# A two-layer attention and feed-forward kernel: the first batch of the second attention moved ahead of the mixture's last batch, all places worked out anew

## The chip, the core and the metric

The kernel runs on one core of one Trainium2 chip. The metric is the time of one execution on the device, in microseconds, from the median of several runs. The work runs on five engines that each have their own queue and meet only through semaphores: TensorE (PE, with PEld for its weight loads), VectorE (DVE), ScalarE (ACT), GpSimd (POOL) and SyncE (SP), which here only issues DMAs.

## What is computed

Four blocks are added onto x, one after the other, each on a layer norm of x:

```python
# x, ctx: (8 batches, 128 tokens, 128 channels)
x = x + L0_xattn(layernorm(x), ctx, ctx)      # attention over channels, 4 heads, twice (global, local)
x = x + L0_ffn(layernorm(x))                  # "mixture": 16 experts weigh q, k, v and the output
x = x + L1_xattn(ctx, layernorm(x), ctx)      # "second attention": 16 heads of 8 channels over 128 tokens
x = x + L1_ffn(layernorm(x))                  # 8 experts (2 best of a router) and a shared one

# L0_ffn, of one batch: rw = weights of the 16 experts for each token
q, k, v = sum_e rw[e] * (h @ {q,k,v}_proj[e])
attn = softmax(causal(q @ k.T / 8)) @ v
out = sum_e (attn * rw[e]) @ o_proj[e]

# L1_xattn, of one batch: for each of 16 heads
out = concat_h softmax(q_h @ k_h.T / sqrt(8)) @ v_h;  out = out @ Wc.T + bc
```

## The kernel before

All data stays in SBUF. Work goes batch by batch (b = 0 to 7), and the last block goes by 28 chunks of 128 hidden rows (14 chunks for each half of the batches). The program is one list for each engine, and each list is made by the same loop over a step counter, `for s in range(LAST)`: a function is emitted on an engine where its place says so. A step is no time: it only orders what one engine does. Waits on semaphores do the rest, and an engine that waits holds everything behind it in its list.

The places come from small functions. `at_mix(b, u)` is step 32 b + u of the mixture of batch b, less `MIX_EARLY[b]`. `at_att(b, u)` is step 8 (35 + 2 b) + u of the second attention of batch b, less `ATT_EARLY[b]`; `at_score` does the same for its first scores. `at_once(u)` is step u, for the rest of the first block. `at_tail` places the router, `at_first` the first two chunks of the feed-forward.

The functions that the text speaks of, in the order in which a batch meets them:

- Mixture. `scale_hidden` (L1099, DVE) multiplies the normalised x with the weights of four experts, `project` (L1476, PE, one at steps 0, 8, ... 248, so 32 of them) makes q, k, v. Then `take_qkv` (ACT), `turn_qk` (L1486, PE), `take_qkT` (L658, ACT), `scores2` (L1491, PE), `softmax2_max` (DVE), `exp2` (L665, ACT), `softmax2_norm` (DVE), `turn_p` (L1500, PE), `take_pT` (L672, ACT), `attend2` (L1504, PE), `take_aT` (L678, ACT), `mix` (L1131, DVE), `project_o` (L1514, PE), `after_mixture` (L1135, DVE), `rstd_of` (L488, POOL), `normalise` (L881, DVE).
- Queries of the second attention. `turn_x3` (L1525, PE), `take_xn3T` (L684, ACT), `project_q` (L1529, PE), `split_q` (DVE), `turn_q` (L1534, PE), `take_qs` (L690, ACT).
- Second attention. `scores3` (L1549, PE, two for each batch), `softmax3` (L1144, DVE, only the maxima), `split_m` (DVE), `mark_queries` (L1559 and L1562, PE), `take_marked` (L705, ACT), `turned_scores` (L1576, PE, two for each batch), `exp3` (L700, ACT, two), `attend3` (L1589, PE), `take_y` (L711, ACT), `turn_y` (L1596, PE), `divide` (DVE), `turn_divided` (L1602, PE), `take_yT` (L717, ACT), `bring_x` (L1611, PE), `project_c` (L1615, PE), `after_attention` (DVE), `take_x3` (L721, ACT), `rstd_of`, `normalise`.
- Router and feed-forward. `turn_x4`, `router`, `turn_w`, `up` (L1657, PE), `silu` (L765 or L769, ACT), `hidden` (DVE), `high_hidden` (ACT), `split_hidden` (L533, POOL), `down` (L1713, PE). Their weights are split into a high and a low part while the mixture runs: `high_weights` (L737 to L739, ACT) and `split_weights` (L533, POOL), one of 14 chunks every 8 steps from step 8 W4.

PSUM has eight banks, PB[0] to PB[7], and mixture and second attention use the same ones: PB[1] holds q and k turned, the mixture's scores and the marked queries; PB[3] holds the turned p, attend2, attend3, turned y and divided y; PB[5] holds project_o and project_c. Waits keep the order in which the two may use them. Before the change every such wait says that all eight batches of the mixture are through with the bank, for instance:

```python
def attend3(b):
    pe.wait_ge(ex_ready, 2 * b + 2)
    pe.wait_ge(vm_ready, b + 1)
    if b == 0:
        pe.wait_ge(aT_ready, NB)
    else:
        pe.wait_ge(yT_ready, b)
```

The two `turned_scores` of a batch write the same pair of banks, so the second waits until `exp3` has read the first.

## Time and profile before

| what | us |
|---|---|
| runs of the kernel before | 238.11, 235.94, 236.2 (median 236.2) |
| the profiled execution, its own time | 236.62 |
| its span, first to last instruction | 234.8 |
| PE busy | 211.8 |
| DVE, ACT, POOL busy | 166.5, 112.5, 95.3 |

### The profile page before, as it was taken

What the parts mean: (1) busy time and instruction counts of PE and PEld (TensorE: products, weight loads), DVE (VectorE), ACT (ScalarE), POOL (GpSimd) and SP (SyncE); (2) the same over time, 40 slices, a digit from 0 to 9 for tenths busy, and PEclk for the clock granted to TensorE, in tenths of its full rate; (3) what the DMA queues carried; (4) which work ended last, traced back from release to release, by engine and by line L of the source; (5) the groups of instructions that cost most, each with busy time, mean ns of one, the idle gap of its engine ahead of it and who ended that gap; (6) DMA issues with size and microseconds to landing.
All of it is one profiled execution on the core that took longest, in us unless ns stands there. A gap on an engine that the chain in (4) does not pass through costs nothing.

```text
span 234.8 us, 4985 instructions
## 1 busy us (share of the span) xinstructions
PE 211.8 (90%) x1767; PEld 180.2 (77%) x1767; DVE 166.5 (71%) x495; ACT 112.5 (48%) x259; POOL 95.3 (41%) x127
## 2 busy tenths in 40 slices
PE   1398669999999999999799999998699999999994
PEld 0356549999999998988579888887577887888872
DVE  3598797669977989858792687865765688265753
ACT  0435432423264462422263777678453745555552
POOL 7143100150096999810411021122336655655660
PEclk9999957999999999999976999999999999999998
DMA  6997000398199953300300000000024430163401
GB/s 188 349 419 228 3 6 0 96 289 155 60 260 245 242 190 89 81 12 0 89 4 0 3 3 0 3 4 0 3 48 89 122 101 6 42 189 133 152 27 45
DMA packets 19256, 23.33 MB, mean 99 GB/s; under 512 B 1792, under 2 KB 12192, under 8 KB 19104
## 3 DMA queue, kind: packets, MB, share of 16 engines
q1 hardware_dynamic: 18896, 22.94, 34.3%
q8 instruction: 14, 0.23, 0.4%
q10 hardware_dynamic: 336, 0.08, 0.2%
q14 instruction: 10, 0.08, 0.1%
HBM read 22.39 MB, written 0.62 MB: 98 GB/s over the span
## 4 chain that ended last, share of the span: by engine, by line
PE 83%; DVE 7%; ACT 3%; DMA 2%; issue 2%; ACTq 1%; POOL 0%; DVEq 0%
PE psum L1476 19%; PE psum L1657 17%; PE psum L1713 8%; PE psum L1514 7%; PE psum L1576 3%; PE psum L1589 3%; PE psum L1549 3%; DMA kv<-kv_dram 2%; PE psum L1386 2%; PE psum L1342 2%; PE psum L1491 1%; PE psum L1534 1%; PE psum L1562 1%; PE psum L1596 1%; PE psum L1504 1%
## 5 line engine op out<-in xcount | busy, mean ns | idle before, releaser
L488 POOL TENSOR_TENSOR rstd<-ve,m 128x1 f32<-128x1 f32 (+1 forms) x20 | 14.2, 712 | 96.9 <-DVE ve L872 96.8
L1476 PE MATMUL psum<-wqkv,hm 128*128 128x192 f32 x256 | 47.8, 335 | 0.0
L533 POOL TENSOR_TENSOR qs<-hm,qs 128x512 fp32r<-128x512 f32 (+1 forms) x26 | 33.9, 1302 | 22.3 <-ACT qs L746 22.1
L1476 PEld LDWEIGHTS psum<-wqkv,hm 128*128 128x128 f32 x256 | 42.3, 195 | 0.1
L1144 DVE TENSOR_REDUCE negm<-psum 128x8 f32<-128x1024 f32 x16 | 19.6, 1222 | 7.7 <-PE psum L1549 7.6
L1713 PE MATMUL psum<-qs,wdhi 128*128 128x512 f32 (+1 forms) x56 | 21.8, 401 | 0.1
L1212 DVE TENSOR_TENSOR hm<-hm,psum 128x512 f32<-128x512 f32 x19 | 13.0, 686 | 11.3 <-POOL qs L533 5.0
L700 ACT ACTIVATE exT<-psum 128x1024 f32<-128x1024 f32 x16 | 16.4, 1024 | 7.5 <-PE psum L1576 7.0
L1099 DVE TENSOR_TENSOR hm<-xn2T,exT 128x512 f32<-128x512 f32 x24 | 19.6, 817 | 0.1
L746 ACT ACTIVATE qs<-hm 128x512 fp32r<-128x512 f32 (+1 forms) x28 | 17.5, 627 | 3.3 <-DVE hm L1215 2.0
L765 ACT ACTIVATE psum<-psum 128x512 f32<-128x512 f32 x19 | 11.1, 583 | 16.5 <-PE psum L1657 16.3
L1514 PE MATMUL psum<-wo,mixT 128*128 128x128 f32 x128 | 17.4, 295 | 0.1
L1514 PEld LDWEIGHTS psum<-wo,mixT 128*128 128x128 f32 x128 | 16.6, 209 | 0.3 <-issue 0.2
L1215 DVE TENSOR_TENSOR hm<-hm,psum 128x512 f32<-128x512 f32 x19 | 13.1, 688 | 2.0
L1713 PEld LDWEIGHTS psum<-qs,wdhi 128*128 128x128 f32 (+1 forms) x56 | 10.5, 188 | 3.4 <-DVE qs L1231 0.9
L1131 DVE TENSOR_TENSOR mixT<-aT,rwm 128x1024 f32<-128x1024 f32 x8 | 10.5, 1317 | 2.8 <-issue 1.5
L1657 PE MATMUL psum<-x4hi,wahi 128*128 128x512 f32 (+1 forms) x28 | 12.0, 427 | 0.0
L1576 PE MATMUL psum<-qs,ks 32*128 32x128 f32 x128 | 10.8, 287 | 1.1 <-ACT qs L705 0.9
L1713 PE MATMUL psum<-qs,wdlo 128*128 128x512 f32 (+1 forms) x28 | 11.1, 397 | 0.0
L1657 PE MATMUL psum<-x4lo,wahi 128*128 128x512 f32 (+1 forms) x28 | 11.1, 396 | 0.0
L1657 PE MATMUL psum<-x4lo,wbhi 128*128 128x512 f32 (+1 forms) x28 | 11.1, 395 | 0.0
L1657 PE MATMUL psum<-x4hi,wblo 128*128 128x512 f32 (+1 forms) x28 | 11.0, 393 | 0.0
(235 smaller groups left out, 487.8 us busy)
## 6 DMA issues: line engine op xcount, KB each, us to landing
exT<-rw_rows SPq DMA_DIRECT2D x24, 256.0 KB, 4.8
rwm<-rw_rows SPq DMA_DIRECT2D x16, 256.0 KB, 5.8
hm<-ww_rows SPq DMA_DIRECT2D x7, 256.0 KB, 3.3
wqkv<-wqkv_dram SPq DMA_DIRECT2D x1, 1536.0 KB, 10.5
hm<-ww_rows SPq DMA_DIRECT2D x4, 224.0 KB, 3.3
wa<-wa_dram SPq DMA_DIRECT2D x1, 880.0 KB, 12.9
wb<-wb_dram SPq DMA_DIRECT2D x1, 880.0 KB, 13.3
wdn<-wdn_dram SPq DMA_DIRECT2D x1, 832.0 KB, 15.0
```

What stands on the lines that cost most here:

```text
L488: nc.gpsimd.tensor_tensor(dst, src, m16[:, 0:src.shape[1]], ALU.pow).then_inc(signal, 1)
L533: return nc.gpsimd.tensor_tensor(dst, src, hi.bitcast(F32), ALU.subtract)
L700: nc.scalar.activation(exT[:, b % 2, 2 * p:2 * p + 2, :], turned_pair, ACT.Exp).then_inc(ex_ready, 1)
L746: nc.scalar.activation(hhi[0:n, k % 3, :], hid[0:n, k % 3, :], ACT.Copy).then_inc(hhi_ready, 1)
L1099: V.tensor_tensor(hm[:, b % 2, 4 * q:4 * q + 4, :], bc(xn2T[:, b, :], 1, 4), weights, ALU.mult).then_inc(hm_ready, 1)
L1144: V.tensor_reduce(negm[:, b % 2, 2 * p:2 * p + 2, :], score_pair.rearrange("p j (g k) -> p j g k", g=4), AX.X, ALU.max, negate=True).then_ ...
L1215: V.tensor_tensor(hid[:, k % 3, :], hid[:, k % 3, :], PB[gate_bank(k)][:, :], ALU.mult).then_inc(hid_ready, 1)
L1476: last = mm(bank[:, 0:3 * HD], hm[:, b % 2, e, :], wqkv[:, e, :], start=(e == 0), stop=(e == E0 - 1))
L1514: last = mm(PB[5][:, 0:C], mixT[:, r, :], wo[:, r, :], start=(r == 0), stop=(r == E0 // 2 - 1))
L1576: last = mm(PB[turned_score_bank(j)][:, T * g:T * g + T], ks[quarter(j), b, g, :], qs[quarter(j), b, g, :], start=True, stop=True)
L1657: last = mm(bank[0:n, :], w[:, c0:c0 + n], x[:, cols4], start=(j == 0), stop=(j == 2))
L1713: last = mm(bank[:, :], w[0:n, ch, :], h[0:n, k % 3, :], start=(ch == 0 and j == 0), stop=(ch == NCH - 1 and j == 2))
```

## The change

It keeps all instructions and alters their places and some waits. The mixture's last batch (7) and the second attention's first batch (0) change turns in the banks that they share: attention 0 now needs only seven batches of the mixture, and batch 7 of the mixture waits for attention 0 (`turn_qk` for `take_marked`, `turn_p` for `take_yT`, `project_o` for `take_x3`).

```diff
-W4 = 13
+W4 = 16
-MIX_EARLY = (0, 0, 0, 0, 0, -8, 4, -4)
-SCORE_EARLY = (88, 56, 12, 4, 4, 4, 4, 4)
-ATT_EARLY = (0, 0, 0, 0, 0, 0, 0, 0)
+MIX_EARLY = (0, -8, -16, -8, -12, -8, 4, -4)
+SCORE_EARLY = (92, 44, 12, 4, 4, 4, 4, 4)
+ATT_EARLY = (40, 0, 0, 0, 0, 0, 0, 0)
-SECOND_EARLY = 16
+SECOND_EARLY = 8
...
             def exp3(h):
...
                 if h == 0:
+                    act.wait_ge(hm_ready, 4 * NB - 4)
+                if h == 2:
                     act.wait_ge(hm_ready, 4 * NB)
...
             def turn_qk(b):
...
                 if b >= 1:
                     pe.wait_ge(s2_ready, b)
+                if b == NB - 1:
+                    pe.wait_ge(qm_ready, 1)
                 else:
                     pe.wait_ge(partsT_ready, 1)
...
             def turn_p(b):
...
+                if b == NB - 1:
+                    pe.wait_ge(yT_ready, 1)
                 pe.wait_ge(pn_ready, b + 1)
...
             def project_o(b):
...
+                if b == NB - 1:
+                    pe.wait_ge(x3_ready, 1)
                 pe.wait_ge(mix_ready, b + 1)
...
             def mark_queries(b):
                 if b == 0:
+                    pe.wait_ge(s2_ready, NB - 1)
+                else:
                     pe.wait_ge(s2_ready, NB)
-                else:
                     pe.wait_ge(qm_ready, b)
...
             def attend3(b):
...
                 if b == 0:
+                    pe.wait_ge(aT_ready, NB - 1)
+                else:
                     pe.wait_ge(aT_ready, NB)
-                else:
                     pe.wait_ge(yT_ready, b)
...
             def bring_x(b):
                 if b == 0:
+                    pe.wait_ge(x2_ready, NB - 1)
+                else:
                     pe.wait_ge(x2_ready, NB)
-                else:
                     pe.wait_ge(x3_ready, b)
...
-                    if s == at_att(b, 40):
+                    if s == at_att(b, 42):
                         attend3(b)
...
-                    if s == at_tail(hf, 128, 176):
+                    if s == at_tail(hf, 108, 174):
                         turn_w(hf)
```

Some sixty places (the number u in `at_...(b, u)`) change in the same way as the last two. The mixture of batches 1 to 4 comes 8 to 16 steps later, and that of batches 5 to 7 stays; attention 0 comes 40 steps earlier; in the tail `mark_queries(7)` now stands ahead of `router(0)`, `turn_w(0)` ahead of `bring_x(6)` instead of behind `project_c(7)`, and on ACT `router_softmax(0)` stands ahead of `take_yT(5)`. On POOL, the mixture's `rstd_of` for batch 4 now stands ahead of the last three `split_weights`; before it stood behind all 14.

**The order on PE behind the last `project`.** First the list before, from `project_o(6)` to the second `turned_scores(0)`. L1514 is project_o, L1525 turn_x3, L1529 project_q, L1559 and L1562 mark_queries, L1500 turn_p, L1549 scores3, L1576 turned_scores, L1504 attend2, L1534 turn_q.

```order
L1514 MATMUL psum<-wo,mixT 128x128 x8
L1525 MATMUL psum<-ident,xna 128x128
L1529 MATMUL psum<-wattn,xn3T 128x128
L1559 MATMUL psum<-qs,identr 128x512
L1562 MATMUL psum<-identr,msp 128x128 x4
L1500 MATMUL psum<-ident,pn 128x128
L1549 MATMUL psum<-ks,qs 128x128 x8
L1576 MATMUL psum<-qs,ks 128x128 x8
L1504 MATMUL psum<-pT,v 128x128
L1534 MATMUL psum<-ident,qsp 128x128 x4
L1549 MATMUL psum<-ks,qs 128x128 x8
L1576 MATMUL psum<-qs,ks 128x128 x8
```

Now the list of the changed kernel, whose PE lines are some ten numbers higher, from the first `turned_scores(0)` to `turn_divided(0)`: L1585 is turned_scores, L1510 attend2, L1495 scores2, L1542 turn_q, L1522 project_o, L1599 attend3, L1533 turn_x3, L1606 turn_y, L1537 project_q, L1612 turn_divided, L1506 turn_p.

```order
L1585 MATMUL psum<-qs,ks 128x128 x8
L1510 MATMUL psum<-pT,v 128x128
L1495 MATMUL psum<-qkT 128x128
L1585 MATMUL psum<-qs,ks 128x128 x8
L1542 MATMUL psum<-ident,qsp 128x128 x4
L1522 MATMUL psum<-wo,mixT 128x128 x8
L1599 MATMUL psum<-exT,vm 32x128 x16
L1533 MATMUL psum<-ident,xna 128x128
L1606 MATMUL psum<-ident,ysb 128x128 x4
L1537 MATMUL psum<-wattn,xn3T 128x128
L1612 MATMUL psum<-ident,yq 128x128
L1506 MATMUL psum<-ident,pn 128x128
```

Before, `mark_queries(0)` and the rest of attention 0 came behind `project_o(6)`; now both `turned_scores(0)` come ahead of it, and `attend3(0)`, `turn_y(0)` and `turn_divided(0)` ahead of `turn_p(7)`.

**The order on ACT at the same place.** Before, from `take_qs(4)` on: L690 is take_qs, L658 take_qkT, L665 exp2, L684 take_xn3T, L705 take_marked, L672 take_pT, L700 exp3, L678 take_aT.

```order
L690 ACTIVATE qs<-psum 128x512
L658 ACTIVATE qkT<-psum 64x256
L665 ACTIVATE pn,den<-s,nmx 128x128
L684 ACTIVATE xn3T<-psum 128x128
L705 ACTIVATE qs<-psum 128x512
L672 ACTIVATE pT<-psum 128x128
L700 ACTIVATE exT<-psum 128x1024
L678 ACTIVATE aT<-psum 128x128
```

In the changed kernel, from `take_xn3T(4)` on: L684 is take_xn3T, L658 take_qkT, L702 exp3, L678 take_aT, L690 take_qs, L713 take_y, L665 exp2, L719 take_yT, L672 take_pT.

```order
L684 ACTIVATE xn3T<-psum 128x128
L658 ACTIVATE qkT<-psum 64x256
L702 ACTIVATE exT<-psum 128x1024
L678 ACTIVATE aT<-psum 128x128
L702 ACTIVATE exT<-psum 128x1024
L690 ACTIVATE qs<-psum 128x512
L713 ACTIVATE ysb<-psum 128x512
L665 ACTIVATE pn,den<-s,nmx 128x128
L684 ACTIVATE xn3T<-psum 128x128
L719 ACTIVATE yT<-psum 128x128
L672 ACTIVATE pT<-psum 128x128
```

`take_qkT(7)` no longer stands behind `take_qs(4)`, and both `exp3(0)` and `take_y(0)` now stand ahead of `exp2(7)`.

## Rows read from the trace of the kernel before

**Rows 1.** The page's part 1: busy time of each engine.
```profile
PE 211.8 (90%) x1767; PEld 180.2 (77%) x1767; DVE 166.5 (71%) x495; ACT 112.5 (48%) x259; POOL 95.3 (41%) x127
```

**Rows 2.** Busy time by stretch: stretch, length, busy and instructions of each engine, granted clock.
```profile
core 0: us, PE busy (x) PEld busy (x) DVE busy (x) ACT busy (x) POOL busy (x), PEclk, DMA share, GB/s
24.00:38.70 14.70, 10.60 (x58) 9.08 (x59) 11.54 (x53) 4.76 (x11) 1.01 (x1) 0.65 0.01 3
38.70:106.00 67.30, 67.30 (x480) 63.21 (x479) 53.94 (x154) 26.86 (x105) 37.33 (x59) 1.00 0.59 150
106.00:120.60 14.60, 12.55 (x110) 10.57 (x108) 11.70 (x33) 5.47 (x16) 3.50 (x6) 1.00 0.16 37
120.60:127.40 6.80, 6.43 (x32) 5.82 (x30) 3.42 (x9) 1.79 (x3) 0.00 (x0) 0.50 0.00 1
127.40:134.00 6.60, 6.33 (x118) 5.37 (x116) 4.08 (x10) 4.80 (x7) 0.84 (x2) 1.00 0.01 2
134.00:158.00 24.00, 23.64 (x348) 20.50 (x349) 17.68 (x48) 18.28 (x31) 3.95 (x10) 1.00 0.01 2
158.00:176.00 18.00, 15.43 (x150) 12.03 (x150) 12.08 (x50) 11.11 (x23) 5.82 (x8) 1.00 0.08 15
176.00:232.00 56.00, 55.52 (x251) 44.02 (x249) 35.53 (x70) 30.16 (x55) 32.49 (x25) 1.00 0.31 91
```

**Rows 3.** PE's instructions in order of time: start, us, line, count, idle time before.
```profile
105.72 1.47 PE L1476 MATMUL psum<-wqkv,hm 128*128 128x192 f32 x8
...
112.62 0.48 PE L1491 MATMUL psum<-qkT 64*128 64x128 f32 x2 [0.95 <-ACT qkT L658]
...
159.54 0.66 PE L1576 MATMUL psum<-qs,ks 32*128 32x128 f32 x8 [0.65 <-ACT qs L705]
...
165.58 1.08 PE L1589 MATMUL psum<-exT,vm 128*32 128x128 f32 x32 [1.01 <-ACT yT L717]
```

**Rows 4.** The chain that ended last, in order of time: start, us, what.
```profile
113.18 2.04 PE psum L1514 x16
...
117.44 0.59 PE psum L1549 x8
...
123.36 3.52 PE psum L1514 x16
...
132.98 1.01 PE psum L1589 x32
...
143.50 0.59 PE psum L1576 x8
...
145.87 0.42 PE psum L1611 x2
146.28 0.22 PE psum L1615 x2
```

**Rows 5.** ACT's instructions in order of time, same columns as rows 3.
```profile
111.71 0.60 ACT L690 ACTIVATE qs<-psum 128x512 fp32r<-128x512 f32 x1 [0.16 <-PE psum L1534]
112.20 0.37 ACT L658 ACTIVATE qkT<-psum 64x256 f32<-64x256 f32 x1
...
118.78 1.02 ACT L700 ACTIVATE exT<-psum 128x1024 f32<-128x1024 f32 x1 [0.67 <-PE psum L1576]
...
128.84 0.60 ACT L711 ACTIVATE ysb<-psum 128x512 f32<-128x512 f32 x1
```

**Rows 6.** DVE's costliest groups from 70 to 98 us: xcount, busy, mean ns.
```profile
L1099 DVE TENSOR_TENSOR hm<-xn2T,exT 128x512 f32<-128x512 f32 x13 | 11.8, 905 | 0.0
L1131 DVE TENSOR_TENSOR mixT<-aT,rwm 128x1024 f32<-128x1024 f32 x3 | 4.4, 1467 | 1.5 <-issue 1.5
```

**Rows 7.** The same view from 99 to 122 us.
```profile
L1131 DVE TENSOR_TENSOR mixT<-aT,rwm 128x1024 f32<-128x1024 f32 x3 | 3.7, 1221 | 0.3 <-ACT aT L678 0.3
```

**Rows 8.** POOL's last low part of the weights, from the instructions in order of time.
```profile
98.02 0.90 POOL L533 TENSOR_TENSOR wdlo<-wdn,wdhi 96x128 fp32r<-96x128 f32 x1
```

More of the change, by code:

```diff
@@ L782, in _ @@
                     take_ks(4)
-                if s == at_once(8):
+                if s == at_once(0):
                     take_ks(5)
-                if s == at_once(16):
+                if s == at_once(0):
                     take_ks(6)
-                if s == at_once(24):
+                if s == at_once(30):
                     take_ks(7)
-                if s == at_once(16):
+                if s == at_once(32):
                     take_x1(1)
-                if s == at_once(17):
+                if s == at_once(3):
                     wide_marks()
-                if s == at_once(40):
+                if s == at_once(50):
                     take_xn2T(1)
-                if s == at_once(88):
+                if s == at_once(84):
                     take_rwT(1)
                 for b in reversed(range(NB)):
+                    if s == at_mix(b, 30):
+                        take_qkv(b)
                     if s == at_mix(b, 32):
-                        take_qkv(b)
-                    if s == at_mix(b, 40):
                         take_qkT(b)
-                    if s == at_mix(b, 58):
+                    if s == at_mix(b, 54):
                         exp2(b)
-                    if s == at_mix(b, 74):
+                    if s == at_mix(b, 66):
                         take_pT(b)
@@ L807, in _ @@
                         take_aT(b)
[L808 removed]
+                    if s == at_mix(b, 118):
                         take_xn3T(b)
[L810 removed]
+                    if s == at_mix(b, 134):
                         take_qs(b)
[L812 removed]
+                if s == at_once(64):
                     gate_exp(1)
@@ L1256, in _ @@
                     channel_softmax(1)
-                if s == at_once(1):
+                if s == at_once(0):
                     turn_heads(1)
-                if s == at_once(16):
+                if s == at_once(20):
                     after_channels(1)
-                if s == at_once(24):
+                if s == at_once(36):
                     normalise(xnb, 1, HALF, NB, 4, xn2_ready)
-                if s == at_once(24):
+                if s == at_once(26):
                     norms(1)
-                if s == at_once(48):
+                if s == at_once(56):
                     gate(1, 0)
-                if s == at_once(56):
+                if s == at_once(58):
                     gate(1, 1)
-                if s == at_once(64):
+                if s == at_once(66):
                     gate(1, 2)
-                if s == at_once(72):
+                if s == at_once(66):
                     gate(1, 3)
-                if s == at_once(80):
+                if s == at_once(68):
                     gate(1, 4)
                 for b in range(NB):
-                    if s == at_score(b, 4):
+                    if s == at_score(b, 0):
                         softmax3(2 * b)
-                    if s == at_score(b, 14):
+                    if s == at_score(b, 12):
                         softmax3(2 * b + 1)
@@ L1725, in _ @@
                     turn_keys(4)
-                if s == at_once(8):
+                if s == at_once(0):
                     turn_keys(5)
-                if s == at_once(16):
+                if s == at_once(24):
                     turn_keys(6)
@@ L1731, in _ @@
                     turn_keys(7)
-                if s == at_once(16):
+                if s == at_once(22):
                     attend_channels(1)
-                if s == at_once(40):
+                if s == at_once(48):
                     turn_x2(1)
-                if s == at_once(48):
+                if s == at_once(52):
                     gate_logits(1)
-                if s == at_once(88):
+                if s == at_once(82):
                     turn_rw(1)
@@ L1750, in _ @@
                         project_o(b)
+                    if s == at_mix(b, 120):
+                        turn_x3(b)
                     if s == at_mix(b, 122):
-                        turn_x3(b)
-                    if s == at_mix(b, 126):
                         project_q(b)
-                    if s == at_mix(b, 140):
+                    if s == at_mix(b, 136):
                         turn_q(b)
```

59 lines of the change are left out of this document (28 added, 31 removed).

## Prediction

> **What bounds the kernel now.** I read the busy times first: PE 211.8 of 234.8 us, DVE 166.5, the others half or less [rows 1]. So the end is set by PE's work and by the time in which PE waits or runs slowly. Then the busy time by stretch [rows 2]: from 38.7 to 106 us (30 of the 32 `project`) and from 176 us on PE is never or hardly idle (67.30 of 67.30, 55.52 of 56.00). A reordering can gain nothing there, and loses only if another engine falls behind. Three stretches are left.
>
> 1. From 24 to 38.7 us PE is busy 10.60 of 14.70 us at a mean clock of 0.65. The change leaves the code ahead of the loop as it is and alters little in these steps.
> 2. From 106 to 134 us, between the last `project` and the steady second attention: PE waits 2.05 + 0.37 + 0.27 = 2.7 us, and from 120.6 to 127.4 its clock is 0.50, that is 1.2 GHz. One `project_o` takes 3.52 us there against 2.04 earlier [rows 4].
> 3. From 158 to 176 us, router and first chunks: 18.00 - 15.43 = 2.6 us idle. The largest waits are 0.65 for `take_marked(7)` and 1.01 for `take_yT` [rows 3].
>
> Between these, 134 to 158 us, PE is busy 23.64 of 24.00. So the change must be judged by stretches 2 and 3.
>
> **Up to the last `project`.** Before, it starts at 105.72 [rows 3]. Three of the four `scores3` of batches 0 and 1 had been done by then, after the change two, so one piece of 0.59 [rows 4] moves behind: the last `project` starts at about 105.13. The mixture of batches 1 to 4 is 8 to 16 steps later there, but its work on PE is the same, and other work fills the place. The cover for this is DVE: from 38.7 to 106 it is busy 53.94 of 67.30, and while POOL splits weights it is slower: `mix` takes 1.47 against 1.22 us without it [rows 6, 7]. POOL's last split ended at 98.9 [rows 8]. It will now end at about 110: `rstd_of` for batch 4 must wait for `project_o(4)`, which I place at 101, and three chunks of about 1.8 us, an `rstd_of` and an `add_bc` follow. So `mix(5)` and the last `scale_hidden` run at the slow price (0.905 us) [rows 6]. I count it in the waits below, and take 0 for the stretch itself; if the cover fails, each late `scale_hidden` shows as a wait of PE of some tenths.
>
> **Stretch 2, the work.** Before, from 105.72 to the end of `attend3(1)` at 132.98 + 1.01 = 133.99 are 28.3 us. Of these 2.7 are waits, and the slow clock costs half of the 6.80 - 0.37 us that PE was busy under it, 3.2 us. At full clock 22.4 us of work are left. After the change the same span of the list holds one more `scores3` (0.59), and `bring_x(0)` and `project_c(0)` come ahead of `attend3(1)` (0.42 + 0.22) [rows 4]: 23.6 us. With W for the waits and K for the clock, `attend3(1)` ends at 105.13 + 23.6 + W + K = 128.7 + W + K. The kernel before has come equally far at 133.99 + 0.64 = 134.6. So the difference is W + K - 5.9.
>
> **The waits W.** I set PE's new list out in order, with these prices, beside the lists of ACT and DVE with theirs. One wait of before goes: `scores2(7)` waited 0.95 us [rows 3], as `take_qkT(7)` (0.37) stood behind `take_qs(4)` (0.60) on ACT [rows 5]; it no longer does. But attention 0 brings its own chain without the company of other batches:
> - `mark_queries(0)` waits for `split_m(0)`, which stands behind `mix(5)` at the slow price: 0.3.
> - The second `turned_scores(0)` waits until `exp3` has read the banks (1.02) [rows 5], with only `attend2(6)` and `scores2(7)` between: 0.6.
> - `project_o(6)` waits for `mix(6)`, behind `softmax3(3)` and `split_q(4)` on DVE: 0.4.
> - `turn_y(0)` stands all but directly behind `attend3(0)` and waits for `take_y` (0.60) [rows 5]: 0.7. Behind it on ACT stands `exp2(7)`, though its input is there, and `take_xn3T(5)`, so `project_q(5)` waits 0.4 more.
> - `turn_divided(0)` 0.2, then `turn_p(7)`, by the new wait on `yT_ready`, 0.45: behind it stand `scores3(4)` and all the rest of PE, which need nothing of it.
> - `turn_q(5)`, `turn_x3(6)`, `project_o(7)` (`mix(7)` behind `softmax3(4)`, `after_attention(0)` and `split_m(1)` on DVE; the new wait on `x3_ready` is over by then), the next `turned_scores`: 0.15, 0.3, 0.5, 0.15 and 0.35.
>
> The sum is 4.5 us, an estimate worked out from those rows; hops of 0.04 to 0.1 us may be off, so I keep 3.5 to 5.5. The lower bound for a list that did what it is meant to would be the 2.7 of before. So the change removes one long wait and adds several short ones, +1.8 us net.
>
> **The clock K.** Before, PE's clock fell at 120.6 after a stretch with 12.55 of 14.60 us busy, its longest wait 0.95 us. By my placing, the new list from 106 to 120.6 has waits of 0.3, 0.6, 0.4, 0.7, 0.4, 0.2 and 0.45, that is 3.05 us against 2.05, the most of it at its end. So I expect the fall again, at about the same time and for as long: 6.8 us at half rate lose 3.4 us. The later waits of the list (0.15, 0.3, 0.5, 0.15, 0.35) vanish under the slower PE, as the other engines don't slow down: K = 3.4 - 1.4 = 2.0. If it lasts half as long, 1.7 - 0.7 = 1.0. The bounds are 0 (no fall) and what the start of the kernel shows: 14.70 us at a mean of 0.65 are 10.3 us at half rate, 5.15 us, less some 2.2 of waits, K = 2.9.
>
> Stretch 2 then gives 4.5 + 1.0 to 2.0 - 5.9 = -0.4 to +0.6, and I take +0.1.
>
> **Stretch 3.** `mark_queries(7)` ahead of `router(0)` ends the 0.65 wait. On the other side `attend3(6)` needs `take_yT(5)`, which now stands behind `router_softmax(0)` on ACT, and that waits for the router's maxima on DVE: 0.7 for 0.65. `take_yT(6)` still stands behind the first `silu`, about 1.0 as before. `turn_divided(7)` now stands ahead of `up(1)` and waits 0.8 for `divide(7)`, where `up(1)` used to cover; `turn_w(0)` out of the way early gives some of it back. Before 2.6 us idle, now 2.0 to 3.4: I take -0.2 for the stretch with a range of -0.7 to +0.8. From `up(4)` on all is as before and PE-bound.
>
> The sum against the profiled execution is 236.62 + 0.1 - 0.2 = 236.5; the profile lies 0.4 above the median 236.2, so by the median the forecast is 236.1, in round numbers 236.0. A measurement of this kernel can tell about 1% (2.4 us) from no change.
>
> **The rivals.**
> - *The clock does not fall.* K = 0 gives -1.4 - 0.2 = -1.6: 234.6. With W at 3.5 and the tail at its best it is 233.1, beyond 1%. For it: the new waits are each shorter than the 0.95 that goes. Against it: their sum is larger, and before it was no long wait either that led to the fall.
>   The Trainium skill, "TensorE: Matmul & The Clock Gate", section "HAM oscillation — how this bites in real kernels", has the clock fall after long idle gaps of PE. By that rule neither list would lose the clock, and this case would follow. The trace does not agree: the clock fell to 0.50 at 120.6 with no wait over 0.95 us ahead.
> - *The planner's list does better than mine.* W stays at the 2.7 of before and the clock holds: 2.7 - 5.9 = -3.2 in stretch 2, 236.2 - 3.2 - 0.2 = 232.8. For it: attention 0 and the chains of batches 5 to 7 are independent, so there is work to fill with. Against it: the list puts `turn_y(0)` where only one small turn stands between it and its `attend3`.
> - *Slower.* The thin stretch makes the clock fall sooner and stay low as long as at the start (10.3 us): 4.5 + 2.9 - 5.9 = +1.5, with the waits at 5.5 +2.5, with the tail at its worst +3.3: 237.7 to 239.5. It decides as soon as PE's idle time between 110 and 120 is over 3 us. For it: 0.7, 0.4, 0.2 and 0.45 follow one another within 4 us. Against it: `project_o(6)` and `attend3(0)`, 2.8 us without a wait, come right before.
>
> **How the numbers follow.** The forecast 0.42, within 1%. The clock holds 0.20, of which 0.07 is beyond 1%. The better list 0.22, all beyond. Slower 0.16, of which 0.13 is beyond. So faster 0.29, same 0.42 + 0.13 + 0.03 = 0.58, slower 0.13. The range that leaves 2 in 10 out goes from 232.8 to 238.2; the forecast's own range is 235.0 to 237.2.
>
> **What the changed profile would show.** The last `project` at about 105.1 with no PE wait ahead of it; POOL's last split near 110 and `mix(5)` at 1.4 us; no wait of `scores2(7)`; waits of PE on `exp3`, `take_y` and `take_yT` of batch 0 of 0.4 to 0.7 us; the clock at 0.50 for some 6.8 us from about 120; `attend3(1)` ending at 133.2 + 1.0 to 2.0; 2.0 to 3.4 us idle in the tail. The forecast is wrong if the clock stays at 1.00 from 106 on, if PE waits for `scale_hidden` before 105 us, or if the waits behind the last `project` sum to 3 us or less.

## The result, and the profile after

| kernel | median, us | lowest to highest | ratio to the kernel before |
|---|---|---|---|
| before | 236.41 | 235.94 to 238.11, 4 runs | 1 |
| changed | 241.14 | 240.38 to 256.72, 4 runs | 1.0179 [1.0123, 1.0235] |
| changed, measured again (f1 below) | 240.86 | 235.95 to 257.43, 12 runs | 1.0048 [0.9978, 1.0119] |

The change makes the kernel slower, by 4.7 us in the first comparison and by 3.6 us between the medians of the second. Medians are over all executions, while the ratios leave out those over 1.5% above the kernel's fastest, so the two need not agree: the low ratio of the second row rests on three of the 12 executions (235.95 and 236.38 us at a mean granted clock of 0.985, 238.64 us at 0.971). That spread is a part of the story.

The profiled execution took 241.07 us, its span is 239.3 us (before 236.62 and 234.8). The page's busy times, to be held against [rows 1]:

```profile
PE 217.7 (91%) x1766; PEld 183.8 (77%) x1767; DVE 165.1 (69%) x495; ACT 111.7 (47%) x259; POOL 93.5 (39%) x127
```

The instructions are the same, yet PE is busy 5.9 us longer: 4.5 us of span, and 1.4 us less idle. DVE, ACT and POOL are not busier. So it is not that PE waits more; it is busy for longer with the same work. Now busy time by stretch, the counterpart of [rows 2], with the tail cut where the clock changes:

```profile
core 0: us, PE busy (x) PEld busy (x) DVE busy (x) ACT busy (x) POOL busy (x), PEclk, DMA share, GB/s
24.00:38.70 14.70, 11.68 (x56) 10.12 (x57) 10.49 (x49) 3.67 (x8) 1.01 (x1) 0.55 0.02 3
38.70:106.00 67.30, 66.42 (x468) 62.61 (x468) 52.67 (x156) 27.28 (x106) 32.06 (x51) 1.00 0.57 150
106.00:134.00 28.00, 25.36 (x259) 21.15 (x260) 20.61 (x53) 11.87 (x29) 8.12 (x18) 1.00 0.08 20
134.00:158.00 24.00, 24.00 (x350) 20.10 (x340) 16.87 (x41) 16.91 (x28) 3.52 (x9) 1.00 0.01 2
...
161.50:169.00 7.50, 7.24 (x54) 6.04 (x55) 3.44 (x21) 4.10 (x6) 0.55 (x1) 0.54 0.01 2
```

The clock holds at 1.00 behind the last `project`, where it was at 0.50 from 120.6 to 127.4 before. Instead it is at 0.50 for some 3.4 us longer at the start (0.55 on average against 0.65), and for 6.8 us near 162. The marks of PE, to be held against [rows 3]:

```profile
106.46 1.47 PE L1478 MATMUL psum<-wqkv,hm 128*128 128x192 f32 x8
...
133.41 1.08 PE L1599 MATMUL psum<-exT,vm 128*32 128x128 f32 x32
...
161.76 1.79 PE L1599 MATMUL psum<-exT,vm 128*32 128x128 f32 x32 [0.63 <-ACT yT L719]
...
170.16 1.08 PE L1599 MATMUL psum<-exT,vm 128*32 128x128 f32 x32 [0.84 <-ACT yT L719]
...
173.46 0.33 PE L1612 MATMUL psum<-ident,yq 128*128 128x128 f32 x1 [0.85 <-DVE yq L1167]
```

L1599 is `attend3`, here of batches 1, 6 and 7; it took 1.79 us at the half clock and 1.08 at the full one. And the piece that shows what the forecast missed, in the steady second attention, first before, then after. L1549 and L1557 are `scores3`, L1576 and L1585 the second `turned_scores` of the batch, L1611 and L1622 `bring_x`.

```profile
145.03 0.44 PE L1549 MATMUL psum<-ks,qs 32*128 32x128 f32 x4
145.21 0.33 PE L1576 MATMUL psum<-qs,ks 32*128 32x128 f32 x2
145.31 0.28 PE L1549 MATMUL psum<-ks,qs 32*128 32x128 f32 x2
145.37 0.27 PE L1576 MATMUL psum<-qs,ks 32*128 32x128 f32 x2
145.42 0.27 PE L1549 MATMUL psum<-ks,qs 32*128 32x128 f32 x2
145.48 0.38 PE L1576 MATMUL psum<-qs,ks 32*128 32x128 f32 x4
145.80 0.49 PE L1611 MATMUL psum<-xr,ident 128*128 128x128 f32 x2
```

```profile
145.37 0.66 PE L1557 MATMUL psum<-ks,qs 32*128 32x128 f32 x8
145.96 0.49 PE L1622 MATMUL psum<-xr,ident 128*128 128x128 f32 x2
146.37 0.66 PE L1585 MATMUL psum<-qs,ks 32*128 32x128 f32 x8
146.96 0.49 PE L1626 MATMUL psum<-wattn,yT 128*128 128x128 f32 x2
```

Before, the two groups of eight 32x128 matmuls, which use different quarters of the array's rows, stand next to each other in the list and run mixed, in 0.77 us for both (145.03 to 145.80). After, `bring_x`, which uses the whole array, stands between them, and each takes its own 0.59 us. `attend3` follows `attend3` after 4.95 us before (144.02, 148.96, 153.91) and after 5.54 us now (144.35, 149.89, 155.42).

The Trainium skill, "TensorE: Matmul & The Clock Gate", section "Part 3: Packing small matmuls — row/col tiling", says that matmuls on different row strips of the array run together, but start and end strictly in program order. The rows agree with the running together. They don't agree with the order of the starts: all eight `scores3` stand ahead of the eight `turned_scores` in the list, yet four of them start at 145.31 and 145.42, after the first `turned_scores` at 145.21. So that order isn't what keeps the second group back here; what the rows show is that it starts behind `bring_x` where `bring_x` stands between.

### The profile page after: what moved, and what is told of

It reads as the page before. It is cut to its first block, busy times and chain, and to the rows that moved or that the text cites. A ratio compares the mean times of both kernels' runs of the same rounds, so it can differ in the third digit from the quotient of the medians.

```text
span 239.3 us, 4993 instructions
## 1 busy us (share of the span) xinstructions
PE 217.7 (91%) x1766; PEld 183.8 (77%) x1767; DVE 165.1 (69%) x495; ACT 111.7 (47%) x259; POOL 93.5 (39%) x127
## 4 chain that ended last, share of the span: by engine, by line
PE 83%; DVE 8%; issue 3%; ACT 3%; DMA 2%; ACTq 1%; DVEq 0%
PE psum L1668 17%; PE psum L1478 16%; PE psum L1724 8%; PE psum L1522 6%; PE psum L1599 4%; PE psum L1585 4%; PE psum L1557 3%; DMA kv<-kv_dram 2%; PE psum L1344 2%; PE psum L1606 2%; PE psum L1388 1%; PE psum L1542 1%; PE psum L1622 1%; PE psum L1571 1%; PE psum L1495 1%
## 5 line engine op out<-in xcount | busy, mean ns | idle before, releaser
L702 ACT ACTIVATE exT<-psum 128x1024 f32<-128x1024 f32 x16 | 16.4, 1024 | 9.3 <-PE psum L1585 8.7
L1101 DVE TENSOR_TENSOR hm<-xn2T,exT 128x512 f32<-128x512 f32 x24 | 17.9, 752 | 0.5 <-DMA exT<-rw_rows 0.5
L1522 PE MATMUL psum<-wo,mixT 128*128 128x128 f32 x128 | 15.9, 277 | 0.3 <-DVE mixT L1133 0.3
L1522 PEld LDWEIGHTS psum<-wo,mixT 128*128 128x128 f32 x128 | 15.1, 192 | 0.8 <-issue 0.5
L1133 DVE TENSOR_TENSOR mixT<-aT,rwm 128x1024 f32<-128x1024 f32 x8 | 10.2, 1270 | 4.2 <-ACT aT L678 3.1
L1585 PE MATMUL psum<-qs,ks 32*128 32x128 f32 x128 | 11.0, 292 | 0.6 <-ACT exT L702 0.3
L1668 PE MATMUL psum<-x4hi,wbhi 128*128 128x512 f32 (+1 forms) x28 | 11.2, 401 | 0.0
L1668 PE MATMUL psum<-x4hi,walo 128*128 128x512 f32 (+1 forms) x28 | 11.2, 401 | 0.0
```

What stands on the lines that cost most here:

```text
L702: nc.scalar.activation(exT[:, b % 2, 2 * p:2 * p + 2, :], turned_pair, ACT.Exp).then_inc(ex_ready, 1)
L1101: V.tensor_tensor(hm[:, b % 2, 4 * q:4 * q + 4, :], bc(xn2T[:, b, :], 1, 4), weights, ALU.mult).then_inc(hm_ready, 1)
L1522: last = mm(PB[5][:, 0:C], mixT[:, r, :], wo[:, r, :], start=(r == 0), stop=(r == E0 // 2 - 1))
L1585: last = mm(PB[turned_score_bank(j)][:, T * g:T * g + T], ks[quarter(j), b, g, :], qs[quarter(j), b, g, :], start=True, stop=True)
L1668: last = mm(bank[0:n, :], w[:, c0:c0 + n], x[:, cols4], start=(j == 0), stop=(j == 2))
```

## The experiments

Each row of this table is one profiled execution, cut at four marks read from PE's instructions in order of time: A the start of the last `project`, B 1.01 us after the start of `attend3(1)` (its end at full clock), C the start of `attend3(6)`, D the start of `up(4)`, E the span's end. The last column says where the clock was at 0.50, and for how long. Several have up to 2 us more of that at the span's end, not listed. The profile of i3 is left out: its execution took 246.33 us, 9.7 us over the median of its kernel, with the clock at 0.50 for 27 us between 121 and 152 us.

| profile | A | A to B | B to C | C to D | D to E | clock at 0.50, us |
|---|---|---|---|---|---|---|
| before | 105.72 | 28.20 | 26.21 | 15.97 | 58.70 | start 10.2, from 120.6 6.8 |
| changed | 106.46 | 27.96 | 27.34 | 18.40 | 59.14 | start 13.7, from 162 6.8 |
| f1_after_again | 104.38 | 27.97 | 27.33 | 15.37 | 59.15 | start 6.8 |
| e1_pair_back | 105.44 | 27.98 | 25.94 | 16.73 | 59.11 | start 10.2, from 161 3.4 |
| e2_pair_broken | 107.00 | 25.23 | 27.73 | 15.99 | 58.75 | start 13.7 |
| e3_tail_back | 105.03 | 27.98 | 28.06 | 15.96 | 58.67 | start 6.8 |
| e4_mid_only | 107.61 | 27.97 | 28.00 | 15.89 | 58.83 | start 13.7, from 156 3.4 |
| f2_fill_before | 106.75 | 25.23 | 26.22 | 18.71 | 58.79 | start 13.7, from 159 6.8 |
| f3_fill_tail | 106.67 | 27.97 | 28.66 | 17.36 | 59.24 | start 13.7, from 162 3.4 |
| f4_before_tail | 106.72 | 25.24 | 28.38 | 21.04 | 59.12 | start 13.7, from 158.5 13.7 |
| h1_fill_start | 104.95 | 26.76 | 26.22 | 18.91 | 58.66 | from 120 3.4, from 158 6.8 |
| h2_qkT_ahead | 104.67 | 25.24 | 26.21 | 18.66 | 58.92 | start 6.8, from 156.5 6.8 |
| h3_both | 104.43 | 25.25 | 26.22 | 18.68 | 58.72 | from 156.5 6.8 |
| i1_hold_before | 104.06 | 28.08 | 26.12 | 16.14 | 60.10 | from 118.5 6.8 |
| i2_hold_after | 104.12 | 29.09 | 27.32 | 15.38 | 60.49 | from 113 3.4 |
| j1_full_before | 104.68 | 25.17 | 26.13 | 16.14 | 58.68 | none |
| j2_full_pair | 105.13 | 27.89 | 27.94 | 15.07 | 59.27 | from 132 3.4 |

My theory after the result: the order itself costs about 3 us, and the clock's falls land where they do in each execution. The rival: the order is nearly neutral, and the changed kernel loses by making the clock fall more.

**e1_pair_back.** The changed kernel with the pair together again, all but batch 0.

```diff
-                    if s == at_att(b, 32):
+                    if s == at_att(b, 32 if b == 0 else 28):
                         turned_scores(2 * b + 1)
```

> The changed kernel, with the second turned_scores of batches 1 to 7 on PE 4 steps earlier again, so that it follows scores3 directly and bring_x comes behind both. Theory A (the two sets of small matmuls, on different quarters of the array, ran side by side in the kernel before: 0.77 us for both against 0.59 + 0.59 apart, and the period of a batch went from 4.95 to 5.54 us where bring_x parts them): three batches get 0.5 to 0.6 us back each, so about 1.7 us faster than the changed kernel, 239.4 us, periods of attend3 4.95 us. Theory B (PE is not what sets the period there): the period stays 5.5 us and the time 241.

Median 238.62 us (before 237.09 in the same job), ratio 1.0045 [1.0005, 1.0086]. B to C is 25.94 against 27.33 in f1, both at full clock: 1.4 us.

**e2_pair_broken.** The reverse, in the kernel before, for three batches.

```diff
-                    if s == at_att(b, 28):
+                    if s == at_att(b, 32 if b in (3, 4, 5) else 28):
                         turned_scores(2 * b + 1)
```

> The kernel before, with the second turned_scores of batches 3, 4 and 5 put 4 steps later on PE, so that bring_x parts it from scores3. Theory A: 3 times 0.5 to 0.6 us slower, about 238.1 us, periods of attend3 5.5 us in place of 4.95. Theory B: no change, 236.4.

B to C is 27.73 against 26.21: 1.5 us for three pairs. The whole is 1.0063 [0.9981, 1.0145], too coarse alone. The rows show the same separate groups as in the changed kernel:

```profile
149.21 0.66 PE L1549 MATMUL psum<-ks,qs 32*128 32x128 f32 x8
149.80 0.49 PE L1611 MATMUL psum<-xr,ident 128*128 128x128 f32 x2
150.22 0.66 PE L1576 MATMUL psum<-qs,ks 32*128 32x128 f32 x8
```

Done and undone give the same size, so this term is shown. The medians agree with it less well: 237.29 us in place of the 238.1 expected. The profile also shows the clock at 1.00 all through A to B, in the old order, and with that A to B takes 25.23 us and not 28.20.

**e3_tail_back.** The changed kernel with the router and the first chunks at their old places, in the manner of

```diff
-SECOND_EARLY = 8
+SECOND_EARLY = 16
...
-                    if s == at_tail(hf, 108, 174):
+                    if s == at_tail(hf, 128, 176):
                         turn_w(hf)
```

> The changed kernel with all places of the router and of the first two feed-forward chunks (on every engine) as before the change. Theory T (the new places of the tail make the waits that let the clock fall at 161 us): the clock stays up there, 2 to 3 us faster than the changed kernel, 238.5 us. Theory P (when the clock falls depends on what PE did in the stretch ahead, which is thin in both): it falls in the tail again and the time is within 0.7 us of 241.1.

Median 239.3, 1.0081 [1.0038, 1.0123]. No fall came in the tail of this one profile. C to D is 15.96 as before, D to E 58.67 as before. But `turn_x4(0)` now waits 1.32 us for `normalise`, so B to C grows to 28.06: the `rstd_of` ahead of it had ended at 152.95, but on DVE `normalise` kept its new place, behind the next `softmax3` and `split_m`, and began at 154.93. Of the tail this says only that its new places change D to E by +0.45.

**e4_mid_only.** Pair, tail and the rest of the first block back; the moved attention and the mixture's places stay.

> The changed kernel with the pairs restored and the head and tail places of the kernel before: of the change only the exchange of batch 7 and batch 0 and the places of mixture and second attention are left. If each part costs by itself: 241.1 - 1.7 (pairs) - 1 (head) - 2.4 (tail) = 236.0. If the fall of the clock in the tail stays: 238.4.

Median 239.81, 1.006 [1.0018, 1.0101], above both expectations, so adding up the parts did not give it. Here too `turn_x4(0)` waits 1.3 us for `normalise`. A to B is 27.97, as in every other unfilled profile with the moved attention, whatever stood around it. The 2.7 us over 25.23 belong to the part of the change that is left here: the exchange of attention 0 and batch 7, with the new places of mixture and second attention.

**f1_after_again.** The changed kernel, unaltered.

> The changed kernel once more, unaltered. What it settles is which of its marks are fixed and which move between executions. Theory (the order costs, the clock is added to it): from the last project to the end of attend3(1) 28.0 us again, attend3 periods of 5.54 us in the steady part again, whatever the clock does; the stretch at 0.50 at the start between 6.8 and 13.7 us long; a second stretch at 0.50 near 160 us of 3.4 or 6.8 us. Median 239 to 241 us. Rival (most of the loss was one unlucky placing of the clock's falls): the median of the new executions comes within 1.5 us of the kernel before.

A to B and B to C repeat to 0.01 us. No fall came in the tail this time, and C to D took 15.37 us against 18.40. So the order is fixed and the falls are not. The 12 executions go from 236 us at a mean clock of 0.985, over 238.6 to 240.3 at 0.971, to 241.4 to 241.9 at 0.957, and two took 257 us at 0.886. The kernel before took 235.4 and 236.7 at 0.971 and 237.7 at 0.957 in that job, so at an equal mean clock the changed kernel is 3.6 to 4 us slower on average.

**f2_fill_before.** The kernel before with the 0.95 us wait of `scores2(7)` filled.

```diff
+            def fill(bank, n):
+                for i in range(n):
+                    tr(PB[bank][:, 384:512], wattn[:, 2, :], ident[:, :])
+
             def scores2(b):
+                if b == NB - 1:
+                    pe.wait_ge(x2_ready, NB - 2)
+                    fill(5, 7)
```

> The kernel before, with seven turns of 0.11 us into a free bank put ahead of scores2(7), where PE waited 0.95 us. The turns' results are never read. If short idle times of PE between 106 and 120 us are what brings its clock to 0.50 at about 120, the clock now stays at 1.00 there, and last project to the end of attend3(1) takes 25.2 us as in the run e2_pair_broken, not 28.2; the median comes 1.5 to 3 us below the kernel before. If the fall has nothing to do with that wait, it comes as before in most executions, and the median stays within 0.5 us.

Median 237.28, 1.001 [0.9973, 1.0046]. No fall came at 120, but e2 had none either, and one came at 159 instead, where the first profile had none. The median met the second expectation, but one filled wait settles nothing.

**f3_fill_tail.** The changed kernel with `fill` ahead of `attend3(6)` and `attend3(7)`, into the bank of `project_c`.

> The changed kernel with five turns ahead of attend3(6), which waited 0.63 us for take_yT, and eight ahead of attend3(7), which waited 0.84 us; the turns' results are never read. If these waits bring the clock to 0.50 from 162 to 169 us, it now holds, and attend3(6) to up(4) takes 15.0 to 15.5 us, not 18.4: the median comes 2 to 3.4 us below the changed kernel. If the clock falls whatever PE does in those waits, attend3(6) to up(4) stays at 16.7 to 18.4 us.

Median 241.44, 1.0166 [1.0108, 1.0224]. This one failed as a test: to write that bank, `fill` itself had to wait for `take_x3`, 0.71 us, so it came behind the idle time and not into it.

```profile
162.04 1.33 PE L1590 MATMUL psum<-ident,wattn 128*128 128x128 f32 x5 [0.71 <-ACT xr L723]
163.30 1.08 PE L1606 MATMUL psum<-exT,vm 128*32 128x128 f32 x16
```

**f4_before_tail.** The kernel before with the new places of the router and the first chunks.

> The kernel before with only the changed places of the router and of the first chunks. If the new tail's own waits bring the clock down, it shows a stretch at 0.50 beginning between 158 and 163 us, and attend3(6) to up(4) takes 16.7 to 18.4 us against 15.97; from up(4) to the end 0.4 us more than before. If the fall near 162 us came from the moved attention and the parted pairs ahead of it, it doesn't fall here, attend3(6) to up(4) takes about 15.0 us, and the whole is 0.5 us below to 0.5 us above the kernel before.

Median 242.45, 1.021 [1.014, 1.028]: worse than either kernel. A fall of 13.7 us came from 158.5 on, but that isn't the test that was meant: `turned_scores(14)` waits 2.03 us, as `take_marked(7)` kept its old place and so stands behind the moved `router_softmax(0)` on ACT. The new tail places only fit the new attention places, so this run can't tell what they are worth alone.

**h1_fill_start.** The kernel before with PE's idle time between 20 and 33 us filled.

```diff
-            add_rows(PB[5], R_BP)
-            add_x(1)
+            fill(5, 22)
             sum_queries(1)
+            fill(5, 5)
             turn_x2(0)
+            fill(5, 6)
...
             turn_keys(1)
+            fill(5, 5)
             turn_keys(2)
             turn_keys(3)
+            add_rows(PB[5], R_BP)
...
             turn_rw(0)
+            add_x(1)
```

> The kernel before with PE's idle times between 20 and 33 us filled: 38 turns of 0.11 us into a bank that is not used yet, and the bias rows and x of the second half put into that bank after them, later than before. The turns' results are overwritten, never read. If idle time of PE is what brings its clock to 0.50 at 25 to 29 us in every profile so far, the stretch at 0.50 at the start goes or shrinks to at most 3.4 us, the last project starts at 103 to 104.5 instead of 105.7 to 107.0, and the median is 1.5 to 3 us below the kernel before, if no other fall takes its place. If the fall does not depend on these idle times, it stays 6.8 to 13.7 us long and the time is the same or up to 1 us more.

The fall at the start is gone. That stretch, and the one in which the clock fell later:

```profile
24.00:38.70 14.70, 12.51 (x93) 9.75 (x91) 11.99 (x53) 4.96 (x11) 1.01 (x1) 1.00 0.02 4
...
158.00:176.00 18.00, 16.18 (x128) 12.64 (x129) 9.46 (x35) 9.51 (x19) 4.19 (x5) 0.81 0.04 10
```

All ten other profiles up to here and h2 had 6.8 to 13.7 us at 0.50 at the start; none of the seven filled there (h1, h3, i1 to i3, j1, j2) had any. So idle time of PE brings that fall. But the median is 236.63 us against 236.61, 0.9998 [0.9952, 1.0044]: what the start gave (`project` at 104.95, not the 103 to 104.5 expected, against 105.72) went again in falls at 120 and 158, where 3.4 us of fall cost 1.5 us (A to B 26.76 against 25.23) and at the start 1.1. At the start PE is busy 10.60 of 14.70 us [rows 2], so a slower PE has idle time to use up; that this is the reason is not shown.

**h2_qkT_ahead.** The kernel before, with the one wait ended that the change does remove.

```diff
-                    if s == at_mix(b, 40):
+                    if s == at_mix(b, 40 if b < NB - 1 else 37):
                         take_qkT(b)
```

> The kernel before with take_qkT(7) placed ahead of take_aT(6) and take_qs(4) on ACT, which alone ends the 0.95 us wait of scores2(7), the one wait of this stretch that the change does remove. If that wait was on the path, from the last project to the end of attend3(1) it takes 24.3 to 24.6 us at full clock, not 25.23, and the median is 0.6 to 0.9 us below the kernel before. If other waits grow by as much (attend2(6) for take_aT(6), mark_queries(0) for take_qs(4)), the stretch keeps its 25.2 us.

Median 236.2, 1.0014 [0.9974, 1.0053]. A to B keeps its 25.24 us. `scores2(7)` does not wait, and the next instruction waits 1.09 us for `mix(6)` on DVE:

```profile
110.54 0.48 PE L1491 MATMUL psum<-qkT 64*128 64x128 f32 x2
112.12 1.13 PE L1514 MATMUL psum<-wo,mixT 128*128 128x128 f32 x8 [1.09 <-DVE mixT L1131]
```

So the longest wait of the stretch was worth nothing. It stood ahead of one as long that it hid.

**h3_both.** h1 and h2 together.

> Both edits together, as a candidate that beats both kernels. If each works as its theory says: 2 to 4 us below the kernel before, last project at 103 to 104.5 us, and attend3(1) ended 24.5 us later. If neither matters: within 0.5 us of it.

Median 237.33 us, 0.7 above the kernel before in the same job (236.61) and not 2 to 4 below it. The ratio of 0.9903 [0.9835, 0.9972] rests on 4 of its 12 executions. One execution held the clock at 1.00 throughout and took 232.5 us, less than any execution of either kernel.

**i1_hold_before, i2_hold_after, i3_hold_pair.** h3 with `fill` also ahead of `project_o(6)`, `turned_scores(14)`, `attend3(7)` and `bring_x(7)`; the changed kernel with the start filled as in h1 and `fill` ahead of `attend3(6)`, `attend3(7)` and `turn_divided(7)`; and that one with the edit of e1. The banks are ones whose last reader is through, so `fill` adds no wait that lasts:

```diff
             def attend3(b):
 
                 pe.wait_ge(ex_ready, 2 * b + 2)
+                if b == NB - 2:
+                    pe.wait_ge(mx3_ready, NU)
+                    fill(4, 5)
+                if b == NB - 1:
+                    fill(0, 7)
                 pe.wait_ge(vm_ready, b + 1)
```

> The run h3_both with PE's four longest waits after the start filled too: eight turns ahead of project_o(6), five ahead of turned_scores(14), eight ahead of attend3(7), five ahead of bring_x(7), all into banks that nobody reads then. If idle time of PE brings every fall, the clock now stays at 1.00 nearly everywhere in most executions, attend3(6) to up(4) takes 16.0 us instead of 18.7, and the median is 232 to 234 us, 3 to 4 us below the kernel before and below its own fastest executions. If the falls come anyway, only elsewhere, the median stays at 236 to 237 us.

> The changed kernel with the same filling of the start, and turns ahead of attend3(6), attend3(7) and turn_divided(7) into banks that are free without a new wait. With the clock's falls out of both, the difference to i1_hold_before is the order alone: my theory says 3.4 us (2.7 behind the last project, 1.1 in the steady attention, 0.4 from up(4) on, less 0.2 ahead of the last project and 0.6 in the tail), that is 236 us with the clock held. The rival, that the changed kernel is slower because it lets the clock fall more, says less than 1.5 us between the two.

> The same with the second turned_scores of each batch but the first put back to its place ahead of bring_x. Theory: attend3(1) to attend3(6) 1.4 us shorter than in i2_hold_after (25.9 us against 27.3), and the whole 1.4 us below it, still 2 us above i1_hold_before. If the parted pairs only looked dear because the clock or a wait moved with them, the two have the same median.

Medians 237.77 (0.9948 [0.9892, 1.0003]), 239.36 (1.01 [1.0068, 1.0133]) and 236.66 us (0.9958 [0.9923, 0.9993]), with the kernel before at 237.08. So i1 missed its 232 to 234 us. No fall came in the filled tail; with the old order and tail and no filling there it had come four times in six (f2, h1, h2, h3; not before and e2). A fall that began at 113 or 118.5 took its place, behind waits of 0.24 to 0.37 us that were still unfilled. The pair's term is there in the whole time: 2.7 us between i2 and i3. That is more than 1.4, and the rest has its own row: in i1 and i2, not in i3, PE stands still once for 1.1 us while waiting for nothing that the profile shows, and D to E is 1.4 us longer (60.10 against 58.68 in j1).

```profile
207.28 1.05 PE L1747 MATMUL psum<-ident,xr 128*128 128x128 f32 x8
209.41 0.47 PE L1685 MATMUL psum<-x4hi,wahi 128*128 128x512 f32 x1 [1.08 <-issue]
```

What that is stays open. Between the medians of i1 and i2 lie 1.6 us, where 3.4 were expected for the order and less than 1.5 by the rival. With falls left in both and this standstill in both profiles, that settles neither.

**j1_full_before, j2_full_pair.** i1 with three turns more ahead of `project_q(4)`, (5) and (6); i3 with two to four ahead of `turned_scores(1)`, `project_o(6)`, `turn_y(0)`, `turn_divided(0)` and `turn_p(7)`.

```diff
             def project_q(b):
+                if b == 4:
+                    pe.wait_ge(x2_ready, 5)
+                    fill(5, 3)
+                if b in (5, 6):
+                    pe.wait_ge(aT_ready, b + 2)
+                    fill(3, 3)
                 pe.wait_ge(xn3T_ready, b + 1)
```

> i1_hold_before with three turns each ahead of project_q(4), (5) and (6), where PE waited 0.37 us each time, so that hardly any idle time of PE between 20 us and 176 us is left unfilled. If idle time brings the fall that i1_hold_before had at 118.5 us, the clock is 1.00 from the first to the last but a few us, the mean at least 0.99 in most executions, and the median 232.5 to 234 us. If falls come at about 120 us although PE is hardly idle there, idle time is not the whole cause, and the median stays near 237 us.

> i3_hold_pair with PE's waits of 0.28 to 0.46 us behind the last project filled as well (ahead of turned_scores(1), project_o(6), turn_y(0), turn_divided(0), turn_p(7)). If the clock holds in both, it stays 1.5 to 2.5 us above j1_full_before, which is what the moved attention costs by its order (2.7 behind the last project, less the scores3 and bring_x that it takes over from elsewhere). If the filling alone decides, the two are equal within 0.5 us.

This is a version that beats both kernels. j1 takes 233.46 us (232.66 to 234.79), 0.9865 [0.9826, 0.9904] of the kernel before: 3.2 us faster than it, and 7 us below the changed kernel. The clock by stretch, the counterpart of [rows 2]:

```profile
24.00:38.70 14.70, 12.35 (x91) 9.66 (x90) 12.01 (x52) 5.08 (x12) 1.01 (x1) 1.00 0.01 3
38.70:106.00 67.30, 66.09 (x467) 61.98 (x467) 53.93 (x153) 26.15 (x104) 37.07 (x59) 1.00 0.57 150
106.00:134.00 28.00, 27.31 (x312) 23.48 (x315) 21.26 (x56) 14.72 (x31) 5.54 (x11) 1.00 0.08 21
134.00:158.00 24.00, 23.52 (x361) 20.19 (x361) 17.13 (x58) 18.17 (x31) 4.39 (x9) 1.00 0.01 2
158.00:176.00 18.00, 17.34 (x125) 13.85 (x126) 11.57 (x36) 9.99 (x20) 6.26 (x7) 1.00 0.14 46
```

Five of its six executions have a mean clock of 0.993 to 0.998, against two of the 12 of i1. So filling PE's idle time, down to waits of 0.37 us, takes nearly all falls out of the old order; these are six executions in one job. j2 did not hold it: 241.24 us at the median, 0.9996 [0.9947, 1.0045], with four executions of 236.2 to 237.2 us at a clock of 0.99 and most others of 241 us at 0.96 to 0.97. In its profile a fall came at 132.2, right behind a wait of 0.29 us, one of three that were left from 106 us to there (0.32, 0.24 and 0.29). The same wait, of 0.28 us, brought no fall in the unfilled changed kernel, so it can't be called the cause. The four executions at 0.99 lie 2.8 to 3.7 us above j1 at nearly the same clock, which is more than the 1.5 to 2.5 us expected; from the table, A to B is 2.7 of it.

## Why the prediction was wrong

The difference of the two profiles, 4.5 us, splits into an order part, read between profiles with the same clock in each stretch, and a clock part, the rest of it.

| stretch | order | from | clock in the two profiles |
|---|---|---|---|
| up to A | -0.3 | e1 to before 105.44 - 105.72; f1 to h2 104.38 - 104.67 | +1.0 (106.46 - 105.44) |
| A to B | +2.7 | 27.97 - 25.23 | -3.0 (25.23 - 28.20) |
| B to C | +1.1 | 27.33 - 26.21 | 0 |
| C to D | -0.6 | 15.37 - 15.97 | +3.0 (18.40 - 15.37) |
| D to E | +0.4 | 59.14 - 58.70 | 0 |
| sum | +3.4 | | +1.1 |

Against the steps of the prediction:

- *Up to the last `project`*: -0.59 foretold, -0.3 found. Right in sign. The stretch itself was put at 0, but `turn_qk` now waits 0.69 us for `take_qkv` at 98.84, and `turn_p` 0.19 us at 56.32. The size itself is rough: e3 and f1, both with 6.8 us at half clock, have A 0.65 us apart. It came at 106.46 and not 105.1 because of the longer fall at the start, which differs between executions of one kernel (13.7 us in the first profile of the changed kernel, 6.8 in the second).
- *The waits W*: 23.6 + 4.5 = 28.1 us foretold for this stretch without the clock, 27.97 measured six times. That the sum was met is luck, as both of its terms failed. Here is A to B at full clock in the old order (e2) and in the new one (f1), columns as in [rows 2]:

  ```profile
  107.00:132.23 25.23, 22.54 (x253) 19.25 (x251) 19.39 (x50) 12.03 (x26) 4.36 (x8) 1.00 0.09 22
  104.38:132.35 27.97, 25.32 (x265) 20.92 (x263) 20.90 (x54) 12.17 (x27) 7.70 (x17) 1.00 0.08 20
  ```

  PE's waits are 25.23 - 22.54 = 2.69 us and 27.97 - 25.32 = 2.65 us: they don't grow at all, where W was 4.5 (3.5 to 5.5). The new list has more waits, but none over 0.46 us. The sign of a wrong forecast that the prediction named, waits of 3 us or less, is there. The work that W was added to is 25.3 us and not 23.6. So all of the 2.7 us is busy time of PE. Of it 1.23 us moved in, as foretold (`scores3` 0.59, `bring_x` and `project_c` 0.64); the other 1.5 us are the same matmuls, at full clock, taking longer in their new order. Some 0.5 of that is of the kind that e1 and e2 show: in e2 two pairs of `scores3` and `turned_scores` overlap here, in f1 none. One pair of f1 stands together in the list and still runs apart, since `turned_scores` also waits for `exp3` (L702), in a wait so short that PE counts as busy through it:

  ```profile
  127.79 0.66 PE L1557 MATMUL psum<-ks,qs 32*128 32x128 f32 x8
  128.39 0.66 PE L1585 MATMUL psum<-qs,ks 32*128 32x128 f32 x8
  127.31 1.02 ACT L702 ACTIVATE exT<-psum 128x1024 f32<-128x1024 f32 x1 [2.01 <-PE psum L1585]
  ```

  What the rest of about 1 us is, no run separates; more waits too short to show as idle can be in it. And that "one wait of before goes" counted for nothing (h2): a wait's length is no price, as the next one may hide behind it.
- *134 to 158 us*: this step failed. The prediction read 23.64 of 24.00 us busy and judged by the other stretches alone. Busy time says that PE is not idle, not that its work takes the same time in another order. The places in the diff had it: the second `turned_scores` goes from 28 to 32, behind the next `scores3` and `bring_x`. It costs 1.4 us; B to C should have been 0.64 shorter, for the two pieces that moved ahead, and is 1.1 longer. Some 0.4 us of that is left unexplained.
- *The clock K*: this step failed too, twice. The formula W + K - 5.9 credits the change with the 3.2 us that the fall at 120.6 cost the kernel before. Of the six other profiles with the old order there and at most one wait filled, five have no fall (e2, f2, f4, h2, h3) and one a fall of 3.4 us (h1). The credit was one execution's, not the kernel's. And K was set at 1.0 to 2.0: no profile of the new order without filling had a fall there. In return the changed kernel lost 3.0 us to a fall at 162, which was in no rival.
- *The tail*: -0.2 foretold; at full clock -0.6 to `up(4)` and +0.4 behind it, so -0.2. "From `up(4)` on all is as before" was wrong by that 0.4, which e3 takes back.
- *The rivals*: "the clock does not fall" was what happened behind the last `project`; it gave 234.6 by the same errors. "The planner's list does better" gave 232.8 for waits of 2.7 us and a held clock. Both conditions came true (2.65 us, 1.00), and the time was 8 us off, so it was the work and the credit that failed, not the waits. "Slower" had the right side but the wrong place, 110 to 120 us: there the clock held.

So of the 4.5 us between the profiles, 3.4 are order and 1.1 are the clock. Of the order, the parted pairs, which the prediction put at nothing, are 1.4 and shown by e1 and e2; about 1 us from A to B is located but not explained.

## What to carry to other kernels

Where groups of small matmuls on different parts of the array stand next to each other and both have their inputs, they can run side by side (0.77 us for two of 0.59 here); before moving anything between them, price both orders, even where the engine is already never idle. Check a sum of several terms term by term: here waits and work were both wrong, and their sum right. Take no credit for a fall of the clock that one profile shows: compare stretches at the same clock, over several executions. And PE's idle time can be worth filling with turns into a free bank, if nearly all of it is filled: in h1, h3 and i1 a part of the filling left the median within 0.7 us of the kernel before, and j2, with few short waits left, still lost its clock in most executions.

## What was not expected of the hardware

- The same kernel has the clock at 0.50 in other places from one execution to the next, for 3.4 to 13.7 us each. A fall of 6.8 us costs 3.0 us behind the last `project` and 2.7 to 3.0 in the tail; at the start 3.4 us more of it cost 1.1 (A at 105.72 against 106.8 on average in e2, f2 and f4).
- It fell at 113 us in i2_hold_after with no longer waits of PE behind the last `project` than these two:

```profile
106.93 0.66 PE L1581 MATMUL psum<-identr,msp 128*128 128x128 f32 x4 [0.33 <-DVE msp L1158]
...
112.61 0.68 PE L1595 MATMUL psum<-qs,ks 32*128 32x128 f32 x8 [0.28 <-ACT exT L702]
```

  The Trainium skill's "TensorE: Matmul & The Clock Gate" has, besides the rule on long gaps that the prediction weighed, a section "A second HAM failure mode: psum-queue depth-cycling", by which many very short idle times between groups of matmuls make the clock go up and down. The runs agree with that one in part: j1, with nearly all short waits filled, had no fall until 229 us. But `changed` and f1 have the same two waits as i2 there and six more behind them, and kept the clock at 1.00, so short waits alone don't tell when it falls.
- A standstill of PE of 1.1 us with no releaser at 207 to 209 us in two kernels that differ from others only by added turns (i1, i2). No run here tells its cause.
